# Storing the output of a cross-attention and expert layer: five plain transfers from SP against sixteen indexed ones from GpSimd

## The reference, cut to what matters

```python
x = x + xattn(ctx, layernorm(x), Wq)      # q = x Wq', k = v = ctx Wq', causal softmax over 256 keys
x = x + ffn(layernorm(x), ...)            # second half, below
# ffn, for x_flat of 2048 tokens x 128:
gates = softmax(x_flat @ gate_W)                    # 8 experts
tk_g, tk_i = top_k(gates, 2); tk_g /= sum(tk_g) + 1e-08
cw = sum(one_hot(tk_i) * tk_g)                      # 2048 x 8 weights
out = x_flat
for e in range(8):
    h = relu(x_flat @ W1[e] + b1[e])                # 128 -> 256
    out = out + cw[:, e:e+1] * (h @ W2[e] + b2[e])  # 256 -> 128
```

## Time and profile before

| | |
|---|---|
| time, median of 2 runs | 143.59 us |
| span of the profiled execution, first to last instruction | 142.0 us |
| median time less that span | 1.6 us |
| PE busy | 128.8 us (91%) |
| DVE busy | 107.1 us (75%) |
| ACT busy | 98.0 us (69%) |
| POOL busy | 56.3 us (40%), 66 instructions |
| written to memory | 1.05 MB |

### The profile page before, as it was taken

One profiled execution on the slowest core, in us unless ns is written; L12 is line 12 of the kernel. 1 busy time (PEld: TensorE's weight loads), 2 busy tenths in 40 slices (PEclk: granted clock), 3 DMA queues, 4 the chain that ended last, 5 costly groups with the idle time before them and its releaser, 6 DMA issues. The chain is left out here.

```text
span 142.0 us, 3307 instructions
## 1 busy us (share of the span) xinstructions
PE 128.8 (91%) x1181; PEld 95.9 (67%) x1181; DVE 107.1 (75%) x422; ACT 98.0 (69%) x205; POOL 56.3 (40%) x66
## 2 busy tenths in 40 slices
PE   6789739989999989999999899999998999699992
PEld 2369528567887656867886568787975667567781
DVE  0748989997749799498568897677497994978573
ACT  3136636788894966778949686789867848689940
POOL 6591953033038943303097730330327603333500
PEclk9999985699999999999999999999999999999999
DMA  3998020000002000200020000200000002000002
GB/s 109 314 283 269 10 76 5 0 0 2 0 7 71 0 2 5 74 0 5 0 74 0 7 0 2 78 0 0 2 5 0 0 5 74 0 2 5 0 0 74
DMA packets 9904, 5.54 MB, mean 39 GB/s; under 512 B 504, under 2 KB 9888, under 8 KB 9888
## 3 DMA queue, kind: packets, MB, share of 16 engines
q1 hardware_dynamic: 9744, 5.27, 13.0%
q10 hardware_dynamic: 144, 0.07, 0.2%
HBM read 4.28 MB, written 1.05 MB: 38 GB/s over the span
## 5 line engine op out<-in xcount | busy, mean ns | idle before, releaser
L653 POOL TENSOR_TENSOR h_lo<-h,h_hi 128x512 f16<-128x512 f32 x24 | 27.8, 1159 | 67.1 <-ACT h L536 67.1
L536 ACT ACTIVATE h<-psH,b1T 128x512 f32<-128x512 f32 x64 | 43.4, 686 | 2.7 <-PE psH L368 1.8
L535 ACT ACTIVATE h_hi<-psH,b1T 128x512 f16<-128x512 f32 x48 | 33.0, 687 | 10.3 <-PE psH L368 10.2
L821 DVE SCALAR_TENSOR_TENSOR acc<-psY,weight_y,acc 128x128 f32<-128x128 f32 x125 | 35.1, 342 | 4.2 <-PE psY L389 3.3
L805 DVE TENSOR_TENSOR h_lo<-h,h_hi 128x512 f16<-128x512 f32 x24 | 17.3, 721 | 15.2 <-ACT h L536 15.2
L364 PE MATMUL psH<-x_hi,w_hi 128*128 128x512 f16 x62 | 24.0, 387 | 0.2 <-ACT h L536 0.2
L368 PE MATMUL psH<-x_lo,w_hi 128*128 128x512 f16 x62 | 23.8, 384 | 0.4
L365 PE MATMUL psH<-x_hi,w_lo 128*128 128x512 f16 x62 | 23.8, 385 | 0.0
L389 PE MATMUL psY<-w_hi,h_hi 128*128 128x128 f16 x192 | 22.7, 219 | 0.0
L389 PE MATMUL psY<-w_lo,h_hi 128*128 128x128 f16 x192 | 22.7, 219 | 0.0
L389 PEld LDWEIGHTS psY<-w_hi,h_hi 128*128 128x128 f16 x192 | 15.4, 98 | 3.3
(11 more groups left out here) (211 smaller groups left out, 209.6 us busy)
## 6 DMA issues: line engine op xcount, KB each, us to landing
w_sb<-in_L_ffn_W_dram SPq DMA_DIRECT2D x8, 256.0 KB, 4.5
ctx_sb<-in_ctx_dram SPq DMA_DIRECT2D x4, 256.0 KB, 2.7
x_sb<-in_x_dram SPq DMA_DIRECT2D x1, 768.0 KB, 6.5
out_dram<-acc SPq DMA_DIRECT2D x3, 256.0 KB, 2.2
x_sb<-in_x_dram SPq DMA_DIRECT2D x1, 256.0 KB, 3.5
out_dram<-acc SPq DMA_DIRECT2D x2, 128.0 KB, 1.8
wq_sb<-in_L_xattn_Wq_dram ACTq DMA_DIRECT2D x1, 64.0 KB, 2.7
b_rows<-in_L_ffn_b_dram SPq DMA_DIRECT2D x3, 4.0 KB
```

The costliest lines, as they stand in the source:

```text
L535: nc.scalar.activation(h_hi[:, C * (e % 2) + c, :], psH[c][:, :], ACT.Relu, bias=bias, scale=scale)
L536: nc.scalar.activation(h[:, C * (e % 2) + c, :], psH[c][:, :], ACT.Relu, bias=bias, scale=scale).then_inc(h_ready, 1)
L653: nc.gpsimd.tensor_tensor(h_lo[:, i, :], h[:, i, :], h_hi[:, i, :], ALU.subtract).then_inc(hlo0_ready, 1)
L821: last = nc.vector.scalar_tensor_tensor(out=o, in0=y, scalar=weight_y[:, t, e:e + 1], in1=o, op0=ALU.mult, op1=ALU.add)
```

## The change

No store is issued by SP any more. POOL fills a table `rows` of 128 x 16 integers once, `rows[p, t] = 128 t + p` (an iota). A tile is stored by one indirect transfer issued by POOL: 128 rows of 512 bytes of `acc`, whose row numbers in the output are read from column t of the table. After the instructions of a group, POOL waits until expert 7 of that group is added and issues four such transfers; in the last group each of the four waits for its own tile. At the end POOL waits for all sixteen.

```diff
+    out_rows = out.rearrange("b s d -> (b s) d")
+        rows = sb("rows", [P, TILES], i32)
...
-            def store(g):
-                sp.wait_ge(y_used, Y_FREE + (g + 1) * E)
-                sp.dma_start(out_v[:, bass.ts(g, TG), :], acc[:, bass.ts(g, TG), :]).then_inc(out_done, 16)
-
             next_context(1)
             for g in range(0, GROUPS - 2):
                 next_context(g + 2)
-                store(g)
-            store(GROUPS - 2)
-            for t in range(0, TG, 2):
-                i = (GROUPS - 1) * TG + t
-                sp.wait_ge(y_used, Y_FREE + GROUPS * E - 1 + t + 2)
-                sp.dma_start(out_v[:, i:i + 2, :], acc[:, i:i + 2, :]).then_inc(out_done, 16)
-            sp.wait_ge(out_done, 16 * (GROUPS - 1 + TG // 2))
...
+            nc.gpsimd.iota(rows[:, :], [[P, TILES]], base=0, channel_multiplier=1).then_inc(rows_ready, 1)
+            pool.wait_ge(rows_ready, 1)
+
+            def store_tile(t):
+                pool.indirect_dma_start(out_rows, bass.IndirectOffsetOnAxis(ap=rows[:, t:t + 1], axis=0),
+                                        acc[:, t, :], None).then_inc(out_done, 16)
...
+            def store(g):
+                pool.wait_ge(y_used, Y_FREE + (g + 1) * E)
+                for t in range(g * TG, (g + 1) * TG):
+                    store_tile(t)
+
             for g in range(0, GROUPS - 2):
                 group(g, True, True)
+                store(g)
             group(GROUPS - 2, True, False)
+            store(GROUPS - 2)
             group(GROUPS - 1, False, False)
+            for t in range(TG):
+                pool.wait_ge(y_used, Y_FREE + GROUPS * E - 1 + t + 1)
+                store_tile((GROUPS - 1) * TG + t)
+            pool.wait_ge(out_done, 16 * TILES)
```

More of the change, by code:

```diff
@@ L72, in xattn_moe @@
     out_v = out.rearrange("b s d -> (b s) d").rearrange("(t p) d -> p t d", p=P)
+    x_rows = x.rearrange("b s d -> (b s) d")
+    out_rows = out.rearrange("b s d -> (b s) d")
     w1_v = w1.rearrange("e d h -> d e h")
@@ L203, in xattn_moe @@
         xf_ready, xfT_ps, xhi_ready, xlo_ready = sem("xf_ready"), sem("xfT_ps"), sem("xhi_ready"), sem("xlo_ready")
+        rows_ready = sem("rows_ready")
         base_ready = sem("base_ready")
```

## The result

The changed kernel takes **156.1 us** (median of 2 runs, 155.89 and 156.32), against 143.59 us: a ratio of 1.087 with a 95% interval of 1.082 to 1.093. The forecast was 147.8 us, with a range up to 151.3. Slower was right; the size was wrong by a factor of three: 12.5 us instead of 4.2.

What follows compares the result with a forecast made beforehand. PE was taken to bound the groups, the last store's landing the end. Span 142.0 + 3.4 (tail) + 0.7 (store of group 2) = 146.1 us; with 1.6 us around it, 147.8 us, range 145.2 to 151.3.

Steps and rivals of the forecast that it cites:

- What bounds the kernel, and the two places: PE bounds the groups; store costs show at the end and where stores keep POOL from an h_lo PE needs.
- D: Time one indirect transfer of 128 rows holds POOL, 1.16 us; as a rival: faster by over 2%, chance 0.02.
- 8D - 5.1: Total cost in us for D between 1.0 and 1.33, giving 146.5 to 149.1 us; chance 0.48.
- The argument against a higher price: Against transfers holding POOL longer: even POOL's widest instructions stay near 1.2 us.
- then 1.8 us as before: Kernel end: four transfers in a row, then 1.8 us to the span's end; tail costs 4D - 1.2, +3.4 us.
- Stores of groups 0 and 1: Delayed h_lo of expert 1 still ready 0.7 us before PE needs it: cost 0.
- The collision on L796: Delayed h_lo holds this DVE instruction about 1.1 us, hidden from PE; bounds 0 to 0.5 us a group, taken 0.
- Store of group 2: In group 3 h_lo comes late, but PE's 1.26 us wait for weight_cat absorbs most: +0.7 us.
- The iota, SP's queue, the transfer engines: Iota in POOL's idle time costs 0, SP's removed issues save 0 outside the tail, smaller transfers collide with nothing.
- B: Rival: each transfer holds POOL longer, all three places stall; D of 1.45 gives 151, 1.7 gives 155 us; chance 0.22.
- C: Rival: not slower, POOL issues nearly like SP, only the tail pays; moved DVE collision gains at most 0.75 us; chance 0.28.

Runs made afterwards that it cites:

- E1: The change with groups 0 to 2 stored by SP, so only the last group's four tiles are indexed transfers from POOL: 148.33 us, ratio 1.030.
- E2: The change with the last group stored by SP as before: 151.4 to 151.7 us in three executions, 149.1 in one.
- E8: The change with the indexed stores moved to where POOL is idle and the last group stored by SP: 144.01 us, ratio 1.0023.
- E7: The change with each transfer storing only 64 of its 128 rows: 155.04 us, ratio 1.082.
- E5: The change with stores moved to where POOL is idle, and SP instead of POOL waiting at the end: 148.03 us, ratio 1.031.
- E3: The change with a small POOL write and a wait for it between a group's four transfers and the next h_lo: 151.97 us, ratio 1.056.
- E6: The change with a plain transfer without a table for each tile, in the same places: 153.0 us, ratio 1.067.
- E9: The change with plain transfers, plus a small POOL write and a wait behind each four of them: 150.0 us, ratio 1.041.

## Why the prediction was wrong, step by step

- **What bounds the kernel, and the two places.** Right: the whole loss lies in the tail and where the stores keep POOL (E1, E2, E8).
- **D.** Taken as 1.16 us; measured 1.26 us in steady sequence (0.96 + 0.30); the first of all took 1.22 us, the first of the tail 0.98. By the prediction's own formula, 8D - 5.1, 1.26 us gives 148.6 us. It explains 0.8 of the 8.3 us missed. The row of POOL's ordinary instruction was a good neighbour by luck: the price does not follow the size of the work (E7). The argument against a higher price, that POOL's widest instructions stay near 1.2 us, was a misreading: L673 took 1.50 us in the kernel before, and that D would have given 151.9 us.
- **Tail, "then 1.8 us as before".** This step failed: it took 3.1 us from the last transfer to the end, because the closing DRAIN of POOL stands behind the landing and takes 1.37 us after sixteen transfers; the data themselves had landed 1.3 us after the last transfer. The sum had no term for it. With 0.28 us before the first transfer and 0.1 us of spacing, the tail cost 5.15 us instead of 3.4. E5 recovers 1.0 us. With four transfers in all the DRAIN is 0.39 us (E1), so by that count 1.0 us of the tail's price comes from the twelve transfers of the groups.
- **Stores of groups 0 and 1, "the cost is 0".** This step failed most clearly. The margin of `h_lo` was as computed (PE has it in time). The collision on L796 was seen, but priced as one `h_lo` from its start on, "about 1.1 us", and so hidden. In fact the hold began at least 0.4 us before `h_lo` started, and went on through a second `h_lo` that followed without a break: 2.90 us, which nothing hides. Cost 1.5 and 1.7 us. E3 (2.5 us back in groups 1 and 2 for one small instruction and a wait), E6 and E9 show the hold ahead.
- **Store of group 2, +0.7 us.** Failed in size: 3.7 us. The wait for `h_lo` was forecast at about 2 us and was 2.40. But I let the 1.26 us of the wait for `weight_cat` absorb it, while the same hold made `weight_cat` late as well (0.77 us again), and the granted clock fell behind the long wait (1.6 us), which no step had in it. The waits are 1.9 us longer than before (2.40 + 0.77 - 1.26); with the clock that is 3.5 of the 3.7 us.
- **The iota, SP's queue, the transfer engines.** Right: the iota takes 0.15 us in POOL's idle time; in E8 twelve transfers cost nothing that can be told from noise.
- **The rivals.** B had the sign and size of the loss but not its cause: it wanted D over 1.7 us. C asked that a transfer be cheap; even E6, where it takes 0.54 us, is 6.7% slower. The only rivals with an instruction of DVE in them, C and D, had it as a gain. The Trainium skill, "DMA: Bandwidth & Descriptors", section on the anatomy of one DMA on the GpSimd path, calls descriptor generation small; taken as the time that POOL is held, this does not fit here: POOL was held 0.96 us for each. The port rule of the Trainium skill, "SBUF — State Buffer", "Who interferes with whom", which I cited for a gain, was the loss: there it is said that the one that issues first holds the shared pair. The rows here fit that only if an instruction counts as issued while a transfer before it still runs, or if POOL's rows start later than its work; the runs do not tell these two apart.

Not settled: how much of the loss in group 3 is the clock. The rows of one execution give 1.6 us; the two kinds of execution of E2 differ by 2.3 us, heads included; and its trace of the lower kind has 1.3 us more in group 3 than the change. No run held the clock by itself. Nor is it settled why POOL's DRAIN grows with its transfers.

## What to carry to other kernels

Moving work to an idle engine is priced by what stands behind it in that engine's queue, and by which other engine shares a port with that: ask which two-input or SBUF-to-SBUF instructions of DVE will fall beside the delayed ones, and count a delayed pair as one block. A transfer of 128 rows costs POOL 0.5 us plain and 1.3 us indexed, and half the rows saved only 0.06 us, so few transfers are better than many (larger ones were not tried). Put where POOL waits anyway, they cost nothing measurable; at the end of the kernel each one does. The wait for the last data belongs on an engine whose closing DRAIN is cheap; POOL's grows with every transfer that it issued before.

## What the runs showed of the hardware that was not expected

- An instruction of POOL that stands ready behind a transfer holds DVE off before its own start in the trace: 2.90 us in the change and 2.49 us in E6, against 0.19 and 0.69 us; with a small write and a wait between, 0.19 and 0.69 us (E3, E9). It struck an instruction with one input as well (L805, 2.95 us, both its tensors in SBUF).
- The transfers themselves were not seen to hold DVE: DVE's `h_lo` beside the first ones of a store keeps its 0.69 us (at 60.69 us in the change), and so does the 0.19 us instruction beside the fourth in E3.
- An indexed transfer holds POOL for 0.96 us with 0.30 us of issue (0.90 us for 64 rows); a plain one for 0.54 us.
- POOL's DRAIN at the end took 1.37 us behind the landing with sixteen transfers in the kernel and 0.39 us with four (E1), and in E5 ended 2.0 us after the last transfer; SP's took 7 ns behind the landing in E5.
- Behind the same waits of PE the lower clock lasted for different times: from about 129 to 132.6 us in the change, from about 127.6 to about 134.4 us in E2 (0.50 in between).
